# Two-layer graph kernel: one more block finished beside the gathers, waves and middle turns reordered

## What is computed

```python
h = relu(layernorm(x))
msg = einsum(basis(edge_attr), h[src], weight)          # layer 0, 9 basis functions per edge
x1 = x + segment_mean(msg, dst) + h @ root_w.T + root_b
h = relu(layernorm(x1))
xp = h @ W_gat                                          # layer 1, 8 heads; every node also has a loop to itself
alpha = leaky_relu(a_src[src] + a_dst[dst])
gat = mean_heads(segment_sum(softmax_by_dst(alpha) * xp[src])) + bias
u = layernorm(gat + h)
out = x1 + layernorm(relu(u @ w1 + b1) @ w2 + b2 + u)
```

## Time and profile before

| | us |
|---|---|
| median of three runs | 3253.76 (3248.36 to 3260.42) |
| profiled execution, its time | 3263.96 |
| profiled execution, its span | 3262.2 |
| POOL busy | 2458.8 (75%) |
| PE busy | 2247.2 (69%) |
| DVE busy | 1858.0 (57%) |
| ACT busy | 839.7 (26%) |

### The profile page before, as it was taken

How to read it: one execution, slowest core, us unless ns; L and a number is a source line. 1 busy time by engine, 2 the same in 40 slices (tenths; PEclk the granted TensorE clock), 3 DMA queues, 4 the chain that set the end, 5 groups by cost and what they waited for, 6 DMA issues and landing times.

```text
span 3262.2 us, 33511 instructions
## 1 busy us (share of the span) xinstructions
PE 2247.2 (69%) x10666; PEld 1570.5 (48%) x10666; DVE 1858.0 (57%) x3253; ACT 839.7 (26%) x1614; POOL 2458.8 (75%) x2011
## 2 busy tenths in 40 slices
PE   2787777747777777777777645747767547888740
PEld 1555555525555655565565534534444334454420
DVE  4889889983433433334334322346767567898720
ACT  1333233213322223223222222322222222222210
POOL 7778777887878878787787488888783075878877
PEclk9989889977888778777777766767888667888775
DMA  2333233221111112212111111111110110111100
GB/s 59 85 72 78 68 76 79 53 57 28 38 37 33 39 39 41 40 32 43 37 36 30 24 13 31 25 18 28 21 24 9 45 16 16 40 28 28 35 10 10
DMA packets 116212, 123.93 MB, mean 38 GB/s; under 512 B 70726, under 2 KB 72747, under 8 KB 116070
## 3 DMA queue, kind: packets, MB, share of 16 engines
q0 software_dynamic: 64000, 30.57, 10.0%
q1 hardware_dynamic: 52070, 91.52, 8.8%
HBM read 59.51 MB, written 64.00 MB: 38 GB/s over the span
## 4 chain that ended last, share of the span: by engine, by line
PE 35%; DVE 23%; POOL 22%; issue 11%; ACT 6%; SPq 2%; DMA 1%; DVEq 0%; ACTq 0%; POOLq 0%
POOL ring L430 15%; PE C L546 7%; PE V L534 7%; POOL out_rows L478 6%; PE C L510 5%; PE T L495 3%; DVE region L1595 3%; PE V L795 3%; DVE var L1235 3%; PE C L540 2%; PE C L542 2%; ACT sq L923 2%; DVE region L1587 2%; DVE region L1338 2%; ACT hid L934 2%
## 5 line engine op out<-in xcount | busy, mean ns | idle before, releaser
L430 POOL DMA_INDIRECT ring<-in_x,index x800 | 979.3, 1224 | 244.4 <-issue 243.2
L478 POOL DMA_INDIRECT out_rows<-ring,index_out x400 | 496.7, 1242 | 278.3 <-DVE ring L1407 158.9
L1235 DVE TENSOR_REDUCE var<-sq 125x16 f32<-125x512 f32 x325 | 220.7, 681 | 791.9 <-ACT sq L923 791.4
L452 POOL DMA_INDIRECT x_table<-region,index_out x400 | 483.3, 1208 | 152.4 <-issue 121.0
L430 POOL DMA_INDIRECT ring<-x_table,index x400 | 496.5, 1241 | 124.5 <-issue 123.9
L534 PE MATMUL V<-xT,w_q 128*128 128x500 f32 x600 | 369.0, 766 | 74.2 <-ACT hid L934 41.0
L923 ACT ACTIVATE sq<-C 125x512 f32<-125x512 f32 x300 | 179.4, 598 | 903.5 <-PE C L546 527.0
L510 PE MATMUL C<-center,xT 128*125 128x128 f32 x1400 | 246.2, 335 | 104.9 <-DVE hrow L1257 70.0
L546 PEld LDWEIGHTS C<-w_c,hid 128*125 128x125 f32 x2400 | 313.5, 215 | 0.0
L546 PE MATMUL C<-w_c,hid 128*125 128x32 f32 x2400 | 312.2, 293 | 0.0
L495 PE MATMUL T<-ident,hrow 125*128 125x125 f32 x1000 | 190.1, 328 | 164.0 <-DVE hrow L1251 139.0
(11 more groups left out here) (250 smaller groups left out, 3143.8 us busy)
## 6 DMA issues: line engine op xcount, KB each, us to landing
ring<-in_x,index POOLq DMA_INDIRECT x800, 3.3
nodes<-in_x SPq DMA_DIRECT2D x25, 500.0 KB
x_table<-nodes SPq DMA_DIRECT2D x25, 500.0 KB
x_plain<-nodes SPq DMA_DIRECT2D x25, 500.0 KB
nodes<-x_plain SPq DMA_DIRECT2D x50, 250.0 KB
out_rows<-nodes SPq DMA_DIRECT2D x50, 250.0 KB
x_table<-region,index_out POOLq DMA_INDIRECT x400, 2.6
ring<-x_table,index POOLq DMA_INDIRECT x400, 2.7
```

What stands on the lines that cost most here:

```text
L430: pool.indirect_dma_start(out=ring[0:P, j, s * F:(s + 1) * F], out_offset=None, in_=table, in_offset=bass.IndirectOffsetOnAxis(ap=index[0: ...
L452: pool.indirect_dma_start(out=x1_table[:, :], out_offset=bass.IndirectOffsetOnAxis(ap=index_out[0:P, j, s:s + 1], axis=0), in_=rows_out[0: ...
L478: pool.indirect_dma_start(out=out[:, :], out_offset=bass.IndirectOffsetOnAxis(ap=index_out[0:P, j, s:s + 1], axis=0), in_=ring[0:P, j, s * ...
L1235: v.tensor_reduce(unit(var, k), slots(squares(k)), AX.X, ALU.add).then_inc(var_ready, 1)
```

## The change

It does four things.

1. **B turns.** PE runs n1's product before those of e3, e4, e1 and e2, `hidden` in two halves apart from each other, and `back_product` last. DVE runs n2, n1, then the edge stages, then n3's finish. ScalarE (ACT) follows the same order.
2. **D waves.** Units run one per wave in waves 0 to 16, through four slots, in place of three per five waves. The early softmax is spread over waves 10 to 13, with its row moves placed in the next wave among other work. x chunks run in waves 14 to 23, woven into the wave instead of behind it. x block 1's tail and carry are done here too.
3. **y block 0** is summed in waves 20 to 24 and finished in waves 21 to 25. SP loads its rows from wave 11 and wave 16 on. `y_first` becomes `y_second`, the same with y block 1. The rounds after it are `e_block` (2, None), (3, 2), (4, 3), (None, 4).
4. **Scatters** read their rows from `diff` and their indices from `scatter_to`, without copies into `ring` and `index_out`.

The core of the diff:

```diff
-UNIT_AT_D = (0, 1, 2)
-X_FROM = NJ * EARLY + 3
+D_SLOTS = (7, 8, 9, 6)
+JOIN_AT = NJ * EARLY
+X_FROM = JOIN_AT + 4
+Y_FROM = X_FROM + NJ + 1
+def wave(w):
+    at = {stage: w - lag for stage, lag in (("n3", 2), ("n2", 1), ("n1", 0)) if 0 <= w - lag < UD}
+    if X_FROM <= w < X_FROM + EARLY * NJ: at["x"] = w - X_FROM
+    if Y_FROM <= w < Y_FROM + NJ: at["y2"] = w - Y_FROM
+    if Y_FROM < w <= Y_FROM + NJ: at["y3"] = w - Y_FROM - 1
+    if w in (X_FROM + NJ, X_FROM + 2 * NJ): at["carry"] = (w - X_FROM) // NJ - 1
+    if w == JOIN_AT + 1: at["join"] = 0
+    if w == JOIN_AT + 3: at["join"] = 1
 # SP, in place of e_load after all units
+                if w == JOIN_AT + 1:
...
+                    for k in range(3):
+                        e_load(k, k)
+                if w == UD + 1:
+                    all_stored(range(6, SLOTS))
+                    for k in range(3, NJ):
+                        e_load(k, k)
 # POOL, stage E
+            for c in range(NC):
+                pool.wait_ge(ring_filled, c + 1)
...
+                        out=out[:, :], out_offset=bass.IndirectOffsetOnAxis(ap=scatter_to[0:P, e:e + 1], axis=0),
+                        in_=diff[0:P, e * F:(e + 1) * F], in_offset=None,
 # PE, b_turn
-                    hidden(xT[:, 2, :])
+                    hidden(xT[:, 2, :], (0, 1))
...
+                if "n3" in at:
+                    hidden(xT[:, 2, :], (2, 3))
+                if "n1" in at:
+                    st["n1"] = product(xT[:, 1, :], center[:, :], t_at=t["n1"])
...
-                if "n1" in at:
-                    st["n1"] = product(xT[:, 1, :], center[:, :], t_at=t["n1"])
+                if "n3" in at:
+                    back_product(xT[:, 2, :])
 # DVE, b_turn
+                if "n2" in at: rows_over_std(2, spread(2))
+                if "n1" in at: relu_rows(1, spread(1))
                 if "e2" in at: aggregate(b, b * NJ + at["e2"][0])
...
+                if "n3" in at:
+                    rows = place(at["n3"][0])
+                    finish_rows(rows, rows, spread(3), unit_done)
 # PE, d_wave, after its first transposes
+                if three:
+                    pe.wait_ge(t_done, t["n3"] + 1 + CREDIT)
+                    hidden(xT[:, 2, :], (0, 1))
...
+                if not last:
+                    st["d1"] = product(xT[:, 0, :], center[:, :], t_at=t["d1"], frees=ring_used)
+                if x:
+                    open_sums(c)
+                    x_values(t["x"], k, 0, V)
...
+                if three:
+                    hidden(xT[:, 2, :], (2, 3))
+                if x: x_values(t["x"], k, 1, V)
+                if three:
+                    back_product(xT[:, 2, :])
+                if x:
+                    x_values(t["x"], k, 2, V)
+                    x_values(t["x"], k, 3, V)
 # all engines
-            y_first()
+            y_second()
-            for y in range(1, NB):
+            e_block(EARLY, None)
+            for y in range(EARLY, NB):
                 e_block(y + 1 if y + 1 < NB else None, y)
```

More of the change, by code:

```diff
@@ L371, in _ @@
                 b_turn(NB, h, turn(h, last=True), False)
[L373 to L387, removed]
             def e_load(c, j):
@@ L713, in _ @@
                 b_turn(NB, turn(h, last=True))
[L716 to L747, removed]
             def ends_T(n, event):
@@ L796, in x_values, with y_rows @@
                        start=True, stop=True).then_inc(v_ready, 1)
[L798 to L807, removed]
+            def y_rows(y, j, k):
+                pe.wait_ge(row_ready, y * NJ + j + 1)
+                return transpose(unit(hrow, k))
@@ L811, in _ @@
             pe.wait_ge(f_done, 4 * NU * NB + CREDIT)
[L812 to L821, removed]
-                        carries_T(EARLY, FIRST_JOIN[1])
-                    if X_FROM <= at < X_FROM + EARLY * NJ:
-                        x_early(at - X_FROM)
-            d_turn(None, None, last=True)
+            for w in range(NC + 1):
+                d_wave(w)
             tq.restart(); cq.restart(); vq.restart(); fq.restart()
             tq.depth, cq.depth, vq.depth = 1, 1, 3
-            pe.wait_ge(f_done, 4 * SLOTS * NB + CREDIT)
-            def y_rows(y, j):
-                pe.wait_ge(row_ready, y * NJ + j + 1)
-                return transpose(unit(hrow, NORMED[j % 2]))
+            pe.wait_ge(f_done, 4 * (SLOTS * NB + NJ) + CREDIT)
             def y_hidden(t):
@@ L1081, in y_square, with d_wave, y_second @@
                 square(2, unit(hrow, 1))
-            def y_first():
+            def d_wave(w):
+                at = wave(w)
+                first, last = w == 0, w == NC
+                three = "n3" in at or "y3" in at
+                if three: affine()
+                if "n2" in at: evac(hT[:, 1, :])
+                if not first: evac(hT[:, 0, :])
+                if "x" in at: evac(hT[:, EARLY_T[at["x"] % 2], :])
+                if "carry" in at: x_tail_rows()
+                if "join" in at: ends_rows(EARLY)
+                if "y2" in at: y_square(0, at["y2"])
+                if three: hidden((0, 1))
+                if not first: cq.next()
+                if "n2" in at: square(2)
+                if not last: evac(xT[:, 0, :])
+                if "n1" in at: evac(xT[:, 1, :])
+                if "n2" in at or "y2" in at: root(2)
+                if not last: square(0); root(0)
+                if "x" in at: cq.next()
+                if "n1" in at: square(1); root(1)
+                if "carry" in at: x_carry_rows()
+                if "join" in at: carries_rows(EARLY)
+                if three: hidden((2, 3)); square(3); root(3)
+                if w == JOIN_AT + 1: exps(0, EARLY, 0)
+            tq.restart(); cq.restart(); fq.restart()
+            fq.depth = 2
+            for w in range(NC + 1):
+                d_wave(w)
+            tq.restart(); cq.restart(); fq.restart()
+            tq.depth, cq.depth = 1, 1
+            def y_second():
                 late = NB - EARLY
-                y_square(0, 0)
+                y_square(1, 0)
                 ends_rows(late)
@@ L1113, in y_first @@
                 cq.next()
-            y_first()
+            y_second()
             def e_block(x_block, y_block):
-                x = x_block is not None
+                x, y = x_block is not None, y_block is not None
                 if x:
@@ L1128, in e_block @@
                     if y2: square(3)
-                affine(); hidden(); root(3)
+                if y: affine(); hidden(); root(3)
                 if x: x_tail_rows()
-                square(3)
+                if y: square(3)
                 if x: x_carry_rows()
-                root(3)
-            for y in range(1, NB):
+                if y: root(3)
+            e_block(EARLY, None)
+            for y in range(EARLY, NB):
                 e_block(y + 1 if y + 1 < NB else None, y)
```

430 lines of the change are left out of this document (215 added, 215 removed).

## The result

The changed kernel takes 3218.97 us (median of four runs, 3210.64 to 3221.36) against 3257.09 for the kernel before beside it: a ratio of 0.986, 95% interval 0.983 to 0.989. Forecast were 3160 us with a range of 3122 to 3206. The direction was right; of the 93 us forecast, 38 came, and the time lies above the range. The profiled execution of the changed kernel has a span of 3217.0 us against 3262.2.

The account below looks back on a forecast made before the run. POOL's list plus its waits for late compute was taken as the bound. Terms: 3262.2 - 31 - 6 - 13.5 + 80 - 121.6 = 3170, so -93; applied to the median 3253.8 this gave 3160 us, range 3122 to 3206.

Parts of the forecast that it names:

- Where the span is set: Whole kernel: the span is POOL's list plus its waits for late compute, some 190 us; gains come only from these.
- Term 1: Stage B: the new order of turns removes POOL's waits for x1 at its end; -31 us, bounds 0 and -31.
- the two causes: Stage B: PE's waits of 19.7 us at transposes and 13.9 at a bias matmul go; 0 to 33.6 a block.
- Term 2: Stage D from wave 10 to its end: 420 us in place of 426.2, so -6; bounds -78 and +36.
- the waves stay as empty as before: Rival, stage D from wave 10: DVE share stays 68%, stretch 462 us, kernel 3202 us; chance 0.15.
- Term 3: `y_second`: loses a wait, the scan and part of the carry against `y_first`, 143.8 us from 157.3; -13.5.
- Term 4: Added x-only round (2, None) in stage E: delays everything behind by its full length; +80 us, bounds 68 and 101.
- Term 5: Stage E's scatters: five chunks fewer lie behind the late one, 15 in place of 20; -121.6 us.
- Scatters of 1.9 us: Scatters beside DVE operations with two SBUF inputs: ten chunks could cost 110 us more, yet the sum would hardly move.
- The clock in the x-only round: Rival, x-only round: TensorE at its lower clock takes 17.5 us a chunk; +21, kernel 3181 us; chance 0.08.

Follow-up runs that it names:

- `product_last`: `square_later` with PE's long y product moved to the wave's end in waves 21 to 25, VectorE's row sum and finish behind the x sums: 3191.17 us.
- `square_later`: The changed kernel with ScalarE's square of the y sum moved behind its copies of the gathered chunk in waves 20 to 24: 3205.13 us, ratio 0.981.

## Why the prediction missed

- **Where the span is set.** Right. In every pair of kernels that share the late chunk, the span moved with POOL's first scatter of that chunk, within 2 us.
- **Term 1, turns of stage B (-31).** Right: -26.8 at the first gather of stage D (1839.12 against 1865.96) with no wait over 1.3 us left in stage B; by themselves the turns give -30 there and -32 in the span. Of the 4.2 us that lack, 1.3 are that wait, and 2.8 that POOL was busy longer up to there (1468.4 us against 1465.6). The price of the two causes was not right: a block paced by compute got 43 us shorter, more than the upper bound of 33.6. It made no difference, as the term was capped by POOL's 31.1.
- **Term 2, waves of stage D (-6, to 420 us).** This is the step that failed: 460.3, at the very end of the bounds (462). The work was right (311.4 us of DVE against 312), the share was wrong. Two parts of the step fail, both by runs. First, I took off 31 us for waits of PE "for which the new order has a remedy". The new order puts new waits of 14.1, 8.2 and 19.9 us in their place, at the head of waves 12 to 14; moving these later brought 29.4. And the 12.8 at `x_tail_T` did not go: 12.0 and 14.9 us stand there now. Second, I priced a y chunk at its DVE time, 7.4 us. It cost 14.4 in the waves. Two orders (ScalarE's square before its copies, PE's long product before the x values) were 16.4 us of the 72.2 in the stretch; the other 56 stand against 36.6 of DVE work, and what makes up the difference was not separated. The rival "the waves stay as empty as before" had the right stretch, 462, with 0.15, and its 3202 lacks only the 9 us of the other terms and the 10 of the step from span to median (below). Of the wait that it blamed, the `spread` alone gave nothing when moved, and together with the long product that it waits for 8.7 us; the larger part of the loss lay elsewhere.
- **Term 3, `y_second` (-13.5).** Mis-sized: -9.0 (148.3 against 157.3). Beside the missing 4.5 us stands TensorE's clock: 315 matmuls took 80.1 us at a mean of 0.63, and as many took 72.9 at 0.65 before.
- **Term 4, the added round (+80).** Right: chunk 10 ended at 2849.9, 129.5 us behind `y_second`; less the 49.6 of a round's first finish that is 79.9. What the term lacked is its alternative, since the join alone is so short that its y chunks are no filling of idle time.
- **Term 5 (-121.6).** Right: 15 chunks at 24.2 us.
- **Together.** +4.2, +40.3 and +4.5 from terms 1, 2 and 3 are 49, and 3169 + 49 = 3218 against a span of 3217.0. Against the median the miss is 59, as the forecast also took off 10 us because the profiled execution of the kernel before lay 10 above its median. That of the changed kernel (3218.86) lies at its median (3218.97).
- **Rules weighed.** Scatters of 1.9 us came again in `y_second`, beside DVE's operations of 2.16 us with two SBUF inputs, and were swallowed by the wait before chunk 10 as said; beside the short ones of 0.7 us most stayed at 1.19. The clock in the x-only round was 0.82 and its length 80, so that rival had no part.
- **The range.** It took the causes of loss one at a time. The 42 us of the rival on the waves leave it as soon as 5 us are lost elsewhere, and here these were 9 in the small terms and 10 in the step from span to median.

## What to carry to other kernels

Work moved beside other work costs what its place costs, which here was not its busy time. Five chunks with 37 us of DVE work cost 72 us in waves and 75 to 81 us beside a join that DVE already filled. Where engines run hand-written orders, look in each queue at the first instruction that waits for another engine's long stretch, and at what lies behind it that doesn't need that result: moving such waits later gave 28 us without a change in work. Before an engine is made earlier, look how much of it the next one can use: stage B's compute gained 86 us, of which POOL took 27. Price a round that is added against the rounds it frees and also against the version that leaves it out.

## What the runs showed of the hardware

- **One indirect DMA beside each long scan with both inputs in SBUF is held up for 6 us.** It took 6.26 us at 2531.84 in the changed kernel, and between 5.6 and 7.4 in its variants, in place of 1.2. A gather is held up like a scatter: the kernel before has one of 6.27 us at 2375.53, beside its scan at 2373.60. The scan beside it reads its mask from `cont` in SBUF. Where the same scan reads the mask from a PSUM copy, scatters beside it keep their 1.19 us. The changed kernel, DVE's scan of each kind and one of the four scatters beside the second, which are all alike:

```profile
2529.93 7.12 DVE L1293 TENSOR_TENSOR_SCAN region<-cont,region 125x80 f32<-125x80 f32 x32
...
2895.65 6.97 DVE L1293 TENSOR_TENSOR_SCAN region<-C,region 125x80 f32<-125x80 f32 x32
```

```profile
2896.62 1.19 POOL L507 DMA_INDIRECT out_rows<-region,scatter_to  x1 [0.30 <-issue]
```

  This goes further than the Trainium skill's rule (GPSIMD Engine Reference, section 1, Specifications) that the interfaces are shared: here one DMA instruction spans nearly the whole scan. The PSUM operand was not exchanged in an experiment of its own.
- **The same instructions take a few us more or less, in two ways.** Up to the first gather of stage D, kernels that do not differ until then took 1836.1 (`product_last`) to 1841.2 us (`square_later`). And `y_second` took 148.3 us with PE busy 80.1 at a mean granted clock of 0.63, and 141.6 with PE busy 70.2 at 0.66, as shown above.
